# A two-layer deformable convolution: the second stage's leaky step, transposes and copies by pairs of tiles, and a new seam between stages one and two

## The reference

```python
def _dcnv2(x, w_off, b_off, w, b, k, pad):
    om = conv(x, w_off, pad) + b_off            # 3*k*k channels
    oy, ox, mask = om[:, :P], om[:, P:2*P], sigmoid(om[:, 2*P:])
    sy, sx = oy + base_y, ox + base_x           # pixel + tap - pad
    val = _bilinear(x, sy, sx) * mask           # four neighbours, zero outside
    return einsum('ncphw,ocp->nohw', val, w) + b
h = leaky(bn(_dcnv2(x, w_off1, b_off1, w1, b1, 1, 0)))   # 512 -> 256 channels
h = leaky(bn(_dcnv2(h, w_off2, b_off2, w2, b2, 3, 1)))   # 256 -> 512 channels
return x + h
```

## Time and profile before

| | |
|---|---|
| time, median of three runs | 3176.06 us (3172.43 to 3177.47) |
| profiled execution, its own time | 3181.72 us |
| its span, first to last instruction | 3179.9 us |
| PE, DVE, ACT, POOL busy | 96%, 87%, 79%, 53% of the span |
| stage one / two / three, about | 0 to 304, 304 to 690, 690 to 3180 us |

### The profile page before, as it was taken

The page is one execution under the profiler, slowest core; times in us unless marked ns, Lnnn a source line. Parts: engine busy times, 40 slices in busy tenths (PEclk is TensorE's granted clock), DMA queues, the critical chain, the costliest instruction groups (busy, mean ns, idle before and its releaser), DMA issues.

```text
span 3179.9 us, 52201 instructions
## 1 busy us (share of the span) xinstructions
PE 3045.7 (96%) x15660; PEld 2472.5 (78%) x15660; DVE 2755.8 (87%) x4830; ACT 2510.6 (79%) x4736; POOL 1681.7 (53%) x1701
## 2 busy tenths in 40 slices
PE   6997888989999999999999999999999999999998
PEld 6997445558888888888888888888888888888888
DVE  5545899978999998998999998999989999999987
ACT  3665677778888888888888888888888888888886
POOL 0001444456656666566566666566666665666652
PEclk8999899989999999999999999999999999999999
DMA  8998999999999999999999999999999999999994
GB/s 310 322 339 299 352 349 332 334 332 398 373 357 378 368 362 376 365 365 379 359 370 377 357 372 374 356 381 367 359 379 363 364 368 350 362 362 352 367 347 174
DMA packets 432939, 1124.82 MB, mean 354 GB/s; under 512 B 42908, under 2 KB 173084, under 8 KB 432848
## 3 DMA queue, kind: packets, MB, share of 16 engines
q0 software_dynamic: 244672, 891.09, 75.1%
q1 hardware_dynamic: 116944, 161.19, 14.4%
q10 hardware_dynamic: 71232, 71.57, 6.5%
HBM read 1003.70 MB, written 137.04 MB: 359 GB/s over the span
## 4 chain that ended last, share of the span: by engine, by line
PE 69%; DVE 17%; issue 6%; ACT 5%; DMA 2%; ACTq 1%; DVEq 0%; SPq 0%; POOLq 0%
PE psum_t L1269 49%; PE psum_t L1256 9%; PE psum_t L386 5%; PE psum_t L697 4%; DVE arena L1190 4%; DVE val_first L1198 2%; DVE z_sb L1212 2%; DVE val_lo L1205 2%; DVE arena L835 1%; ACT val_hi L1153 1%; ACT psum_t L1139 1%; DMA arena<-w 1%; ACT z_sb L1162 1%; PE psum_t L682 1%; DVE arena L859 1%
## 5 line engine op out<-in xcount | busy, mean ns | idle before, releaser
L1125 POOL DMA_INDIRECT arena<-table,plan_in x1521 | 1516.2, 997 | 968.6 <-DVE arena L1198 419.0
L1269 PE MATMUL psum_t<-val_hi,w_hi 128*128 128x512 f32 (+2 forms) x3096 | 1240.4, 401 | 1.8 <-ACT z_sb L1162 0.5
L1269 PE MATMUL psum_t<-val_hi,w_lo 128*128 128x512 f32 (+2 forms) x3096 | 1200.2, 388 | 0.0
L1269 PE MATMUL psum_t<-val_lo,w_hi 128*128 128x512 f32 (+2 forms) x3096 | 1196.8, 387 | 0.0
L1139 ACT ACTIVATE psum_t<-arena,plan_in 128x512 f32<-128x512 f32 x1521 | 1044.1, 686 | 138.2 <-DVE arena L1190 133.9
L1190 DVE SCALAR_TENSOR_TENSOR arena<-arena,plan_in,psum_t 128x512 f32<-128x512 f32 x1521 | 1123.1, 738 | 10.6 <-ACT psum_t L1139 10.5
L1269 PEld LDWEIGHTS psum_t<-val_hi,w_hi 128*128 128x128 f32 x3096 | 582.6, 188 | 137.2 <-ACT z_sb L1162 36.2
L1269 PEld LDWEIGHTS psum_t<-val_hi,w_lo 128*128 128x128 f32 x3096 | 581.7, 188 | 121.1
L1205 DVE TENSOR_TENSOR val_lo<-psum_t,val_hi 128x1024 fp32r<-128x1024 f32 (+2 forms) x387 | 465.4, 1203 | 230.4 <-ACT val_hi L1153 230.3
L1269 PEld LDWEIGHTS psum_t<-val_lo,w_hi 128*128 128x128 f32 x3096 | 583.7, 189 | 102.9
L1153 ACT ACTIVATE val_hi<-psum_t 128x1024 fp32r<-128x1024 f32 (+2 forms) x387 | 390.0, 1008 | 281.2 <-PE psum_t L1256 281.0
(11 more groups left out here) (90 smaller groups left out, 2454.7 us busy)
## 6 DMA issues: line engine op xcount, KB each, us to landing
arena<-x SPq DMA_DIRECT2D x90, 512.0 KB, 8.3
table<-arena ACTq DMA_DIRECT2D x42, 896.0 KB, 8.3
out<-arena SPq DMA_DIRECT2D x136, 256.0 KB, 4.7
table<-arena ACTq DMA_DIRECT2D x42, 768.0 KB, 7.1
arena<-x SPq DMA_DIRECT2D x70, 384.0 KB, 6.3
arena<-table,plan_in POOLq DMA_INDIRECT x1521, 6.7
table<-table SPq DMA_DIRECT2D x32, 512.0 KB, 8.8
arena<-w POOLq DMA_DIRECT2D x2, 2304.0 KB, 13.9
```

Source lines behind the costliest of these rows:

```text
L1125: nc.gpsimd.indirect_dma_start(landing(r, i)[:, :], None, rows, bass.IndirectOffsetOnAxis(ap=row.bitcast(u32), axis=0))\
L1269: last = nc.tensor.matmul(psum_acc[:, oc, 0:n], a[:, w, oc * P:(oc + 1) * P], b[:, r % 2, kt, 0:n], start=(w == 0 and a is w2_hi and b is ...
```

## The change

Six edits, all in stage two or at its border with stage one.

1. `activate`, `transpose_h` and `copy_h_t` work on pairs of tiles (0,1), (2,3), ... (10,11) of a chunk, and on tile 12 alone. The pair's transposes lie side by side in one PSUM bank.
2. `place` has six instructions: the two steps that add and subtract the rounding constant are one. The tap offsets are in the bias row that `turn` multiplies, shifted by half a pixel, and the pixel coordinates come from `where_sb` by broadcast, so `grid` and its DMA per chunk are gone. `hats` has a bias in both Abs.
3. The first four `near` and the first three `add_far` of stage two stand in the last chunk of stage one.
4. `plan(1)` and its `modulation(1)` stand in stage two ahead of tile 6.
5. The table writes of stage one's last chunk are issued by SP.
6. SP loads one more constant (27 numbers, broadcast) at the start.

```diff
+NEAR_AHEAD = 4
+FAR_AHEAD = 3
+PLAN_AT = 6
@@ stage one, on_sync, behind the loads of x
+                for half, (j0, n) in enumerate(HALVES):
+                    sp.wait_ge(y_copied, (CHUNKS - 1) * CHUNK + 6 + j0 + n)
+                    table_writes(sp, table1, y_stage, CHUNKS - 1, half, table1_written[half])
@@ stage one, ACT, chunk(c, ..., last)
                     for j in range(CHUNK):
                         upper(c, j)
                         if j >= 2:
-                            copy_y(c, j - 2)
+                            copy_y(c, j - 2, written=not last)
+                        if last and j >= CHUNK - NEAR_AHEAD:
+                            near(j - (CHUNK - NEAR_AHEAD))
@@ stage one, DVE, chunk(c, ..., last): behind lower(c, j)
+                        if last and j >= CHUNK - FAR_AHEAD:
+                            add_far(j - (CHUNK - FAR_AHEAD))
-                plan(1)
+                return lambda: plan(1)
@@ stage two
             def near_bank(t):
-                at = 512 * (5 + t % 2)
+                at = 512 * (6 if t < NEAR_AHEAD else 5 + t % 2)
+            def pair_bank(pair):
+                at = 512 * (3 + pair % 2)
+                return psum_t[:, at:at + 512].rearrange("p (k n) -> p k n", k=KT2)
@@ near(t) on ACT: waits
-                    if t >= 2:
+                    if 1 <= t < NEAR_AHEAD:
+                        act.wait_ge(lines_ready, t)
+                    if t > NEAR_AHEAD:
                         act.wait_ge(lines_ready, t - 1)
@@ transpose_h on PE
-                    pe.wait_ge(h_ready, t + 1)
-                    if t >= 2:
-                        pe.wait_ge(h_t_ready, t - 1)
-                    for kt in range(KT2):
+                    pe.wait_ge(h_ready, tiles_to(pair))
+                    if pair >= 2:
+                        pe.wait_ge(h_t_ready, tiles_to(pair - 2))
+                    for i in range(n):
+                        for kt in range(KT2):
...
@@ PE's loop
-                    if t < TILES:
-                        transpose_h(t)
+                    if t in PAIR_AT:
+                        transpose_h(PAIR_AT[t])
@@ ACT's loop
-                    if 0 <= t - 2 < TILES:
-                        copy_h_t(t - 2)
+                    if t - 2 in PAIR_AT:
+                        copy_h_t(PAIR_AT[t - 2])
+                    if t == PLAN_AT - 1:
+                        late_modulation()
@@ activate on DVE
-                    dve.wait_ge(sampled1, t + 1)
-                    v = h_buf(c)[:, j, :]
+                    dve.wait_ge(sampled1, tiles_to(pair))
+                    v = h_buf(c)[:, j:j + n, :]
@@ place on DVE
-                    link(nc.vector.tensor_tensor(s, offs[:, 0:n, 0:2 * TAPS], grid_sb[:, c % 2, 0:n, :], ALU.add), at + 1)
-                    link(nc.vector.tensor_scalar(k, s, 0.0, float(HEIGHT - 1), ALU.max, ALU.min), at + 2)
-                    link(nc.vector.tensor_scalar(k, k, -0.5, ROUND, ALU.add, ALU.add), at + 3)
-                    link(nc.vector.tensor_scalar(k, k, ROUND, None, ALU.subtract), at + 4)
+                    yx = where_sb[:, c * CHUNK:c * CHUNK + n, 0:2].unsqueeze(3).to_broadcast([P, n, 2, TAPS])
+                    link(nc.vector.tensor_tensor(s.rearrange("p t (a k) -> p t a k", k=TAPS),
+                                                 offs[:, 0:n, 0:2 * TAPS].rearrange("p t (a k) -> p t a k", k=TAPS),
+                                                 yx, ALU.add), at + 1)
+                    link(nc.vector.tensor_scalar(k, s, -0.5, HEIGHT - 1.5, ALU.max, ALU.min), at + 2)
+                    link(nc.vector.tensor_scalar(k, k, ROUND, ROUND, ALU.add, ALU.subtract), at + 3)
@@ DVE's loop
+                        if t == PLAN_AT:
+                            late_plan()
-                        if t < TILES:
+                        if FAR_AHEAD <= t < TILES:
                             add_far(t)
...
-                        if t:
-                            activate(t - 1)
+                        if t - 1 in PAIR_AT:
+                            activate(PAIR_AT[t - 1])
```

More of the change, by code:

```diff
@@ L57, in pixel_constants @@
     where[1:] = np.stack([y, x, first], -1).reshape(TILES, P, 3)
-    grid = np.zeros((TILES + 1, P, 2 * TAPS), np.float32)
+    tap_at = np.zeros((1, 3 * TAPS), np.float32)
     for k in range(TAPS):
-        grid[1:, :, k] = (y + k // 3 - 1).reshape(TILES, P)
-        grid[1:, :, TAPS + k] = (x + k % 3 - 1).reshape(TILES, P)
-    return where.transpose(1, 0, 2).copy(), grid.transpose(1, 0, 2).copy()
+        tap_at[0, k] = k // 3 - 1.5
+        tap_at[0, TAPS + k] = k % 3 - 1.5
+    return where.transpose(1, 0, 2).copy(), tap_at
 def pieces(first, count):
@@ L192, in deformable_kernel @@
         turner = part(DY)[0:3 * DY + 1, :]
-        minus_one = part(1)
+        plus_half = part(1)
+        minus_half = part(1)
         plus_one = part(1)
@@ L423, in modulation, with chunk @@
                         .then_inc(gate_ready, 1)
-                def chunk(c, first=False, plans=False):
+                def chunk(c, first=False, plans=False, last=False):
                     for j in range(CHUNK):
@@ L448, in on_scalar, with on_vector @@
                 chunk(CHUNKS - 2, plans=True)
-                chunk(CHUNKS - 1)
+                chunk(CHUNKS - 1, last=True)
                 for j in (CHUNK - 2, CHUNK - 1):
-                    copy_y(CHUNKS - 1, j)
-                modulation(1)
-            def on_vector(dve):
+                    copy_y(CHUNKS - 1, j, written=False)
+                return lambda: modulation(1)
+            def on_vector(dve, add_far):
                 link, count = linker(dve, setup)
@@ L519, in plan, with chunk @@
                     assert steps[0] == PLAN_STEPS_1, steps
-                def chunk(c, first=False, plans=False, slabs=()):
+                def chunk(c, first=False, plans=False, last=False, slabs=()):
                     slabs = list(slabs)
@@ L830, in on_vector @@
+                return near, run
             def on_vector(dve, begin_units):
-                dve.wait_ge(bias_ready, 1)
                 def add_far(t):
@@ L1311, in _ @@
             begin_unit, begin_upper, go_on = third_scalar(act)
-            first_scalar(act)
-            second_scalar(act, begin_unit, begin_upper)
+            near, second = second_scalar(act, begin_unit, begin_upper)
+            late_modulation = first_scalar(act, near)
+            second(late_modulation)
             go_on()
@@ L1318, in _ @@
             begin_units, go_on = third_vector(dve)
-            first_vector(dve)
-            second_vector(dve, begin_units)
+            add_far, second = second_vector(dve, begin_units)
+            late_plan = first_vector(dve, add_far)
+            second(late_plan)
             go_on()
```

195 lines of the change are left out of this document (102 added, 93 removed).

## The result

| | before | after |
|---|---|---|
| median (lowest to highest), 7 runs each | 3176.06 us (3171.65 to 3179.53) | 3189.48 us (3187.47 to 3193.23) |
| profiled execution: span | 3179.9 us | 3187.5 us |
| DVE's last `modulate`, the end of stage two | 689.75 us | 661.44 us |
| from there to the end of the span | 2490.2 us | 2526.1 us |

The kernel became slower: ratio 1.0046, 95% interval 1.0036 to 1.0056. I had forecast 3163 and faster. In the profiled executions stage two ended 28.3 us earlier, more than twice the 12.6 us of my sum, and stage three, of which no line was edited, took 35.9 us longer. Four executions of before in group f were in a slower state and are left out of its median.

A forecast was written before the change was run, and what follows sets the result against it. DVE's instructions were taken to pace stage two, with PE through ACT close behind, and PE stage three. Gains of 5.3 + 4.2 + 1 + 2.1 + 0 = 12.6 us from the 3176.06 median gave 3163.5 us, range 3153 to 3174.

The forecast's parts named there:

- a changed length of stage three: Sign of failure: stage three, unedited and bound by PE, was to start earlier or later but stay as long as now.
- a second slow stretch: Rival, stage two: PE idling about 0.8 us ahead of step 7 drops the clock again each chunk; 3182 us, chance 0.08.
- Leaky step by pairs: Stage two, DVE: one 512-column instruction replaces two of 256, saving 0.068 us a pair, 78 pairs, 5.3 us.
- `place`: Stage two, DVE: one instruction fewer saves 0.32 us in 13 chunks, 4.2 us, plus 1 us from L886's excess.
- the excess on L886: In `place`: L886's 450 ns against its neighbour's 280, laid to POOL's gather descriptor; gain 0 to 2 us, taken as 1.
- The broadcast operand: In `place`: `where_sb` as four-dimensional, zero-stride second operand costs 0; at worst 0.1 us a chunk, 1.3 us.
- Seam: Border of stages one and two: first `add_far` in the last chunk let DVE continue without a pause; 2.1 us, bounds 0 to 5.2.
- The turn of 2.8 us: At the stage border: `upper`, `lower`, `add_far`, `near` wait on one another, 2.8 us each for tiles 10 and 11.
- Stalls: Stage two, DVE: clock falls in a third of chunks, 17 us of stalls against 16.7, so gain 0; bounds -7 to +9.
- the clock never falls: Rival, stage two: stalls shrink to 0.5 us a chunk, 20 us less, 3156 us; chance 0.15.
- the one of 4.1: Stage two, DVE: a single 4.1 us stall in the waits of before, left unchanged in the forecast.
- remark on work in bursts: Stage two, PE: bursts with waits between start at the low clock, which speaks against clumping transposes; no size of its own.

The follow-up runs named there:

- group f: Follow-up runs on a chip with a slower stage three, each timed beside the kernel before, which took 3444.31 us; after as it is took 3442.95 us, 0.9990.
- group h: Follow-up runs on a chip like the first, each timed beside the kernel before, which took 3173.73 us; after as it is took 3189.10 us, 1.0045.
- g1: After with 24 no-ops ahead of VectorE's stage-three loop, first near and add_far again behind stage one's last chunk and the late plan ahead of them: 3447.55 us, 0.9951.
- f4: After with 24 no-ops ahead of VectorE's stage-three loop, and leaky step, transposes and copies tile by tile instead of by pairs: 3430.03 us.
- g2: After with 24 no-ops ahead of VectorE's stage-three loop, and two rounding steps in `place` again instead of the fused one: 3455.71 us, 0.9968.
- h3: The kernel before with 231 VectorE no-ops in stage one, moving its stage-three loop to beginning 1453: 3210.24 us, 1.0117 of before.
- h2: After with 24 VectorE no-ops, so its stage-three loop begins where it did before the change: 3151.92 us, 0.9926 of before.
- f2: After with 24 VectorE no-ops ahead of its stage-three loop, on a chip with a slower stage three: 3426.80 us, 0.9937 of before.
- group e: Follow-up runs that moved VectorE's stage-three loop by no-ops, on a chip with a slower stage three; the kernel before took 3464.99 us there.

## Why the prediction was wrong

The step that failed stands in its first paragraph: "nothing of it is edited, so it only starts earlier or later", said of stage three. It starts 28 us earlier and runs 36 us longer, because the edits ahead of it moved VectorE's loop by 24 instructions. No row of the kernel before shows this as a cost, for it had none; what could be read there is that its list of queues has one for instructions (63 packets). The prediction had named a changed length of stage three as what would refute it, with no mechanism, and gave slower 0.08 for another one (a second slow stretch), which did not come.

Step by step, for what it did argue, by medians of group h: after with the no-ops is 3151.92 against 3173.73, so 21.8 us less where the sum had 12.6. The sizes below are from single traces.

- *Leaky step by pairs, 5.3 us*: right. From one L898 to the next instruction is 0.60 us, and two tiles with their step take 3.49 us (311.10 to 314.59 in g1) in place of 2 x 1.78, six times a chunk.
- *`place`, 4.2 + 1 us*: the removed instruction right; the excess on L886 was mis-sized. The excess is gone in every chunk, 0.45 - 0.28 = 0.17 us: 2.2 in place of 1 over 13 chunks. f4, with single tiles, has it again (L919, 0.45 us). POOL's descriptor as its reason stays open: in g2 a rounding step begins 0.57 us behind that of POOL (456.88 to 457.45), L886 did so by 0.59 us (441.69 to 442.28), and the one in g2 takes 0.28 us. That a second scalar costs nothing, as the prediction has it, the traces show: L885, with two, and L887, with one, take 0.28 us each.
- *The broadcast operand, 0*: right (0.40 us for L914).
- *Seam, 2.1 us*: 3.2 us. The turn of 2.8 us was measured at 2.72 to 2.76 (copies at 294.31, 297.07, 299.79). In before's profiled execution a DMA held copy 6 until 295.84; in after's until 292.01, in more than half of the later runs not at all, so the forecast hung on an event that comes and goes.
- *Stalls, 0*: this was mis-sized most. They are 8.1 us less in the first two traces (16.7 and 8.6) and 5.2 us less in group h (11.2 in h3, 6.0 in h2). The gap was right (1.78 against 1.7), its consequence not: I let the clock fall in a third of the chunks, and from 400 to 600 us it fell in one, after a gap of 1.94 us.

5.3 + 4.2 + 2.2 + 3.2 + 8.1 = 23.0 us, or 20.1 with the stalls of group h, against the 21.8 measured. Without the loop's position the case "the clock never falls" (3156, chance 0.15) would have been the nearest one, and 3151.92 lies just under the range. With it 37.2 us come back on top: 15.4 us slower in group h, 13.4 in the first runs.

Two numbers of the prediction don't follow from its own terms. The chance of "faster" is 0.50 + 0.15 + 0.05 + 0.11 = 0.81 by the chances it lists, not 0.68. Stalls of 0.5 us a chunk and the one of 4.1 are 10.6 us, so the lower bound is -6, not -7. For the chunk whose clock stays, rows 8 show the gap, not the 3.4 us behind it; these have a clock of 1.00 too (392.60 to 396.00), so the reading was right.

The prediction's remark on work in bursts, from the Trainium skill, "TensorE: Matmul & The Clock Gate", section "HAM oscillation — how this bites in real kernels", spoke against the pairs. No run here bears that out: f4, with single transposes, has the lower clock of the two (0.97 against 0.99 in f2, 400 to 600 us). The pairs did not lengthen PE's gap behind `place`: it is 1.78 us with them and 1.90 without.

## What to carry to other kernels

An edit ahead of a hardware loop moves the loop, and one of 283 instructions then had the engine idle 4.7 us in each turn. So compare the page's queue of kind "instruction" before and after, and look for idle time "issue" that recurs once a turn; a few no-ops ahead of the loop (24 here, for 37 us) mended it. And where a fall of the clock costs more than the instruction in the gap, as in `place`, read the gap and not the instruction: 0.32 us of DVE were worth 1.8 in most chunks.

## What was unexpected of the hardware

- VectorE idles 4.6 to 4.8 us for each turn of a loop of 283 instructions in two positions (1198 and 1453), and has no such piece once a turn in three others (1222, 1235, 1298). Some five packets of 8.2 KB go with each.
- PE passed on 2.0 of 4.7 us on the first chip, and less, by medians 0.4 us (group e) to 0.9 us (group f), where data came late.
- The chip itself: the same kernel before takes 3174 and 3176 us in two groups of runs, and 3444, 3464 and 3465 in three. The difference is in stage three (2490 against some 2780 us); stage two ends within the same few us on all.
- The clock behind `place`: over the 17 traces, the gap of PE ahead of its first transposes and the granted clock in the 3.4 us behind them. After 1.77 or 1.78 us it stayed at 1.00 in all 97 places; after 1.88 to 1.94 us it fell in 5 of 15; after 2.08 to 2.10 us in 17 of 22; after 2.19 to 2.23 us in 40 of 46. Where it fell it was 0.50 to 0.64. So 0.1 us of gap changes how often the clock falls, and a fall costs 1.2 to 1.5 us a chunk; but gaps of one length went both ways, and what decides between them is open.
